# A four-layer transformer block on one core: every other even unit's copy of the transposed probabilities moves from ScalarE to VectorE

## The reference

```python
x = _L0_cond_ref(...)   # RMS norm, 8 query heads on 1 key head, rotary, softmax, gated MLP (silu)
x = _L1_cond_ref(...)   # layer norm, 16 heads of 32 channels, normalised q and k, MLP (gelu)
x = _L2_cond_ref(...)   # layer norm, 16 query heads on 4 key heads, masked attention, no MLP
x = _L3_cond_ref(...)   # 8 experts of 64 channels, layer norm, silu, output projection
```

```python
mask = outside_window & ~global_visible | future_block
scores = jnp.einsum('bhtd,bhsd->bhts', q, k_exp) / jnp.sqrt(HEAD_DIM)
scores = jnp.where(mask, -jnp.inf, scores)
attn = jax.nn.softmax(scores, axis=-1)
y = jnp.einsum('bhts,bhsd->bhtd', attn, v_exp)
```

## Time and profile before

| | |
|---|---|
| median of three runs | 1913.11 us |
| the profiled execution's own time | 1912.22 us |
| its span, first to last instruction | 1910.4 us |
| TensorE (matmul) busy | 1839.4 us, 96% |
| VectorE busy | 1130.7 us, 59% |
| ScalarE busy | 1026.9 us, 54% |
| GpSimd busy | 819.3 us, 43% |
| mean granted TensorE clock | 0.987 of full speed |
| copies `PT<-B` on ScalarE / VectorE | 160 / 128 |

### The profile page before, as it was taken

How to read it: one execution, slowest core, us unless ns; L and a number is a source line. 1 busy time by engine, 2 the same in 40 slices (tenths; PEclk the granted TensorE clock), 3 DMA queues, 4 the chain that set the end, 5 groups by cost and what they waited for, 6 DMA issues and landing times.

```text
span 1910.4 us, 35240 instructions
## 1 busy us (share of the span) xinstructions
PE 1839.4 (96%) x12840; PEld 1480.8 (78%) x12840; DVE 1130.7 (59%) x3224; ACT 1026.9 (54%) x2482; POOL 819.3 (43%) x1094
## 2 busy tenths in 40 slices
PE   5889999999999999999999999999999999989987
PEld 3678778888888888888788888878886878865565
DVE  5867445643553446543775488586475786476563
ACT  3553433532343445443566467477467765559875
POOL 4666662211112344233778565336443442244330
PEclk9999999999999999999999999999999999989989
DMA  7436787556445544445456534623532354422421
GB/s 246 140 122 215 255 292 257 191 196 221 156 171 176 187 167 144 166 160 183 141 172 226 180 144 144 208 102 126 206 122 85 132 193 172 165 83 90 127 73 56
DMA packets 98651, 314.76 MB, mean 165 GB/s; under 512 B 11568, under 2 KB 13232, under 8 KB 96944
## 3 DMA queue, kind: packets, MB, share of 16 engines
q1 hardware_dynamic: 98480, 312.52, 47.2%
HBM read 242.48 MB, written 66.58 MB: 162 GB/s over the span
## 4 chain that ended last, share of the span: by engine, by line
PE 85%; DVE 5%; ACT 4%; POOL 3%; DMA 2%; issue 2%; SPq 0%; DVEq 0%; POOLq 0%; ACTq 0%
PE B L360 78%; PE B L363 7%; POOL W L378 1%; ACT SS L366 1%; DMA ST<-in_wpack 1%; DVE T L378 1%; ACT GF L366 1%; DVE FB L381 1%; POOL W L375 1%; ACT L366 1%; POOL SS L375 1%; POOL FB L378 1%; DMA Y<-in_adaw 0%; DVE Y L378 0%; ACT FB L366 0%
## 5 line engine op out<-in xcount | busy, mean ns | idle before, releaser
L375 POOL TENSOR_SCALAR SS<-SS,NM 128x256 f32<-128x256 f32 (+1 forms) x640 | 298.7, 486 | 620.1 <-DVE NM L390 619.8
L360 PE MATMUL B<-HM,W 128*128 128x512 f32 x2304 | 532.1, 390 | 1.0 <-DVE HM L381 1.0
L360 PEld LDWEIGHTS B<-HM,W 128*128 128x128 f32 x2304 | 431.7, 188 | 91.8 <-DVE HM L381 1.8
L360 PE MATMUL B<-G,W 128*128 128x512 f32 x1536 | 381.6, 398 | 2.8 <-POOL W L378 2.4
L360 PEld LDWEIGHTS B<-G,W 128*128 128x128 f32 x1536 | 280.9, 188 | 64.2 <-issue 3.1
L366 ACT ACTIVATE SS<-SS,NM 128x256 f32<-128x256 f32 (+1 forms) x512 | 240.2, 472 | 72.8 <-DVE NM L384 72.4
L360 PE MATMUL B<-HA,W 128*128 128x512 f32 x864 | 221.0, 405 | 8.7 <-DVE HA L378 4.7
L360 PEld LDWEIGHTS B<-HA,W 128*128 128x128 f32 x864 | 161.7, 192 | 50.5 <-issue 8.7
L363 PE MATMUL B<-ident,SS 128*128 128x128 f32 x1152 | 166.7, 281 | 11.9 <-POOL SS L375 9.6
L378 POOL TENSOR_TENSOR R<-R,few 128x16 f32<-128x16 f32 (+2 forms) x57 | 120.7, 2121 | 126.2 <-DVE R L375 126.2
L363 PEld LDWEIGHTS B<-ident,SS 128*128 128x128 f32 x1152 | 133.8, 143 | 44.7 <-issue 13.4
(11 more groups left out here) (111 smaller groups left out, 2647.2 us busy)
## 6 DMA issues: line engine op xcount, KB each, us to landing
W<-kept SPq DMA_DIRECT2D x357, 512.0 KB, 4.4
kept<-W SPq DMA_DIRECT2D x119, 512.0 KB, 4.9
ST<-in_wpack SPq DMA_DIRECT2D x139, 256.0 KB, 2.9
Y<-in_adaw SPq DMA_DIRECT2D x12, 1024.0 KB, 6.4
FB<-FB SPq DMA_DIRECT2D x52, 64.0 KB, 2.9
X<-in_xT SPq DMA_DIRECT2D x1, 3072.0 KB, 13.2
out_xT<-X SPq DMA_DIRECT2D x12, 256.0 KB, 3.8
FB<-in_pos SPq DMA_DIRECT2D x4, 256.0 KB, 5.0
```

Source lines behind the costliest of these rows:

```text
L360: return self.real.matmul(*a, **k) if self.real is not None else self
L375: return self.real.tensor_scalar(*a, **k) if self.real is not None else self
```

## The change

In the third layer the one copy of an even unit is ScalarE's where `g` is a multiple of four, and VectorE's otherwise. The 64 units of the layer have 32 even ones; 16 of them (`g` = 114, 118, ... 126, 146, ... 190) change engine. Everything else keeps its engine, and no step changes its place in the list.

```diff
+def by_scalar(g, k):
+
+    if layer(g) == 2 and g % 2 == 0:
+        return g % 4 == 0
+    return (k + (0 if layer(g) else g % 2)) % 2 == 0
@@ values, TensorE
-                            e.wait_ge(*(a_pt if (k + (qt if nh == 2 else 0)) % 2 == 0 else d_pt).of(g + qt, k))
+                            e.wait_ge(*(a_pt if by_scalar(g + qt, k) else d_pt).of(g + qt, k))
@@ copy, VectorE
-                    if (k + (0 if layer(g) else g % 2)) % 2:
+                    if not by_scalar(g, k):
@@ copy, ScalarE
-                    if (k + (0 if layer(g) else g % 2)) % 2 == 0:
+                    if by_scalar(g, k):
```

## The result

The changed kernel takes 1916.26 us (median of 16 runs, 1912.58 to 1921.06), the kernel before beside it 1912.03 us (16 runs, 1907.40 to 1914.43). The ratio is 1.0025, 95% interval 1.0017 to 1.0033: slower by some 4.8 us (the medians lie 4.2 us apart). The prediction was 1914.1 us, with a range of 1910.0 to 1918.5. The time lies in the range, but past the 1915.7 at which the forecast's own case ended, and slower by over 0.2% is the outcome to which I gave 0.18. The range was right; the net of +1.0 us was not.

What follows compares the result with a forecast made beforehand. TensorE, busy 96% of the span, bounds the kernel, so only its waits count. Losses of 1.9 us less gains of 0.9 give net +1.0 us: 1914.1 us expected, 8-in-10 range 1910.0 to 1918.5.

Steps and rivals of the forecast that it cites:

- the forecast's own case: Whole kernel: net -0.5 to +2.5 us with the clock unchanged, range 1912.5 to 1915.7 us, chance 0.60.
- unit 170's 0.1: VectorE would end unit 170's copy at 1721.76, TensorE starts the bank's next use at 1721.70: +0.1 us.
- the prediction's own signs of being wrong: TensorE's waits for VectorE's PT up over 1 us, half-clock stretches differing in number or length, or time outside 1912.5 to 1915.7.
- 166: Unit 166: the copy delays VectorE's two T<-T, for which TensorE's B<-few,T at 1702.75 waits; +0.55 us.
- 174: Unit 174: the copy delays VectorE's three T<-T, for which TensorE's B<-few,T at 1757.42 waits; +0.5 us.
- 170: Unit 170: ScalarE's exponentials, table load and gelus come earlier, shortening TensorE's wait at 1725.65; -0.48 us.
- VectorE's next wait for TensorE swallows the 0.6: At nine units (114, 122, 126, 146, 154, 158, 162, 178, 190) the copy's delay on VectorE was to reach nothing: 0.
- unit 182's "-0.43; if they don't, 0": Earlier gelus bring B<-T,few at 1816.94 forward 0.43 us if transposes waiting for GpSimd's late multiplies fit ahead; otherwise 0.
- unit 150's +0.34: The copy ahead of VectorE's HM row at 1549.73 delays the last HM row and the matmuls on it: +0.34 us.
- Unit 118: The copy leaves some 0.1 us through the masked maxima ahead of a later copy: +0.1 us.
- unit 186's +0.28: VectorE's late FB<-Y,B delays B<-ZH,W at 1834.56 by 0.48 us, partly absorbed in the later ZL wait: +0.28 us.
- Rival 1: TensorE's clock falls once more, likely at 1749 to 1758 or 1710 to 1716: 1918.1 us if long, 1915.5 short; chance 0.22.

Runs made afterwards that it cites:

- eleven: Against the kernel before, the moved copies except those of units 166, 174, 178, 182 and 186 go to VectorE; 1912.49 us, ratio 1.0002.
- last8: Against the kernel before, only the eight late copies, units 162 to 190, go to VectorE; 1914.34 us, ratio 1.0015.
- five: Against the kernel before, only the copies of units 166, 174, 178, 182 and 186 go to VectorE; 1916.61 us, ratio 1.0016.
- only182: Against the kernel before, unit 182's copy alone goes to VectorE; 1910.26 us, one execution.
- load: Against the kernel before, ScalarE keeps all copies and VectorE does an extra unread 128x512 maximum at each of the 16 places; 1915.76 us, ratio 1.0017.
- relief: Against the kernel before, the 16 copies are left out on both engines, with TensorE's waits for them; 1911.77 us, ratio 0.9998.
- pair: Against the kernel before, VectorE gets unit 170's copy in its place and unit 182's behind the cast of Q and the CX row; 1910.94 us, ratio 0.9996.
- only186: Against the kernel before, unit 186's copy alone goes to VectorE; 1913.72 us, one execution.
- the single units: Three kernels, each moving one copy to VectorE against the kernel before: unit 178, 182 or 186; 1913.79, 1910.26 and 1913.72 us, one execution each.
- behind182: Against the kernel before, unit 182's copy alone goes to VectorE, behind the cast of Q, the reciprocals and the CX row; 1914.38 us, one execution.

## Why the prediction was right and wrong

**What bounds the kernel** held. Unit 122's tight bank held, and unit 170's 0.1 came and was swallowed by the wait for GF behind it. Besides that no matmul waited anew for VectorE's PT; two weight loads did, at 1751 and 1815 us, by 0.87 and 0.81 us, and no matmul was late for it. The 11 places of "eleven" together cost nothing that could be measured. That the time lies in the range is in part luck: its upper part was there for one more half-clock stretch between 1700 and 1800 us, which did not come. Two of the prediction's own signs of being wrong came, the time past 1915.7 and half-clock stretches of another length.

**Right in mechanism and size:** 166 (+0.55 said, +0.60 measured, both in last8 and five too), 174 (+0.5, +0.58), 170 (-0.48, -0.47).

**The step that failed first: "VectorE's next wait for TensorE swallows the 0.6".** I counted 178 among the nine units of which I said this. The late instruction there was no maximum of scores but an FB for which ScalarE was waiting already. ScalarE had no slack behind it, and the delay came out 17 us later on TensorE: +0.50 at 1789.20. Following VectorE's queue was not enough; the engine that waits for it had to be followed until it had idle time to spare.

**The second: unit 182's "-0.43; if they don't, 0".** The early side was right (-0.47 in only182). The multiplies were 0.5 late as said, but slower as well, at 0.8 us for 0.37, so they did not "just fit", and the bound "0" left out that a collision can cost. Measured +0.56 in the changed kernel, of which the copy makes 0.30 (only182, five) and VectorE's pause the rest. That it is delay and slowing together is shown by only182, load, relief and pair against each other.

**The third: unit 150's +0.34.** VectorE's delay was sized well (+0.39 in load, 0.3 for the HM rows of the changed kernel). What failed is the condition of the sum, "with the clock as it was": the half-clock stretch began 0.9 us later in the list, and TensorE did not wait for HM at all. It is the one error on the other side, and it is luck: in an execution whose stretch begins as before, the loss is to be expected. Unit 118 was mis-sized: +0.36 for +0.1, and it is VectorE's, since load has it and relief not.

**The fourth: unit 186's +0.28.** The delay ahead of ZH,W is 0.44 to 0.46 us (load, only186, after); I let part of it vanish in the later wait for ZL. That wait did vanish, but the clock stayed low 3.4 us longer.

**The clock.** Rival 1 was one more stretch of half clock between 1700 and 1800. None came: the wait of 0.78 us fell into the stretch that was there and did not lengthen it, and that of 0.66 us brought no new one. What came is longer stretches near 1826 and 1891. The steps of the copies that load, relief and the single units show are 0.36 + 0.60 - 0.47 + 0.58 + 0.50 + 0.30 + 0.45 = 2.3 us; VectorE's pause at unit 182 adds 0.26, and unit 150 up to 0.3 more where the clock leaves it its loss. The ratio says 4.8 us (3.2 to 6.3).

How much of the rest is the clock can be bounded by the mean granted clock that each execution has on record. It averages 0.9838 over the 16 executions of the changed kernel and 0.9849 over the 75 of the kernel before that ran beside the experiments, and their mean times are 4.1 us apart (the 16 of the kernel before that ran beside the changed one, for which no clock is recorded, were 0.7 us faster than those 75). A straight line through all executions, with one slope for all kernels, gives 0.58 us for each 0.001 of clock (standard error 0.07). By it the lower clock makes 0.6 us, and at equal clock the changed kernel is still 3.5 us slower (standard error 0.5) and load, with a mean clock of 0.9857, 3.4 us. By the prediction's price, 0.42 us for each us at half clock, 0.0011 of clock is some 4.1 us at half clock and 1.7 us, and leaves 2.4. So the larger part of the loss is not that the clock was low for longer. The first figure leaves some 1 us that the steps and the pause do not account for, the second nothing; no run here tells which holds. Where a low stretch begins counts too: it gives 0.6 us to the HM rows at unit 150 and takes 0.45 at unit 186.

## What to carry to other kernels

When a copy moves to a less busy engine, price each place by who is queued behind it and follow the delay through the engine that waits for it until it meets idle time that is not waiting for the delayed work itself; 11 of these 16 copies together cost nothing that could be measured, the five others a ratio of 1.0016. Check also what will now run at the same time: a late and an early instruction can meet, and "it just fits" then has a cost above zero. A copy whose place costs something may be free four instructions later in the same queue, as unit 182's was.

## What the runs showed of the hardware

GpSimd's multiply of 128x128 elements (SBUF to SBUF) takes 0.37 us alone and 0.80 to 0.90 us beside VectorE's additions with two SBUF inputs. Both sides can be slowed: VectorE's T<-Y took 0.82 us where it began while a multiply ran (pair, relief), and 0.69 where it began just ahead of one, which then took 0.90 (only182). I had not looked for this in the kernel before, where one multiply of the four shows it.

TensorE's half-clock stretches differ between kernels with the same matmul list: some have one of 3.4 us at 1411, 1710 or 1750 and others none, and near 1826 they have 10.2 to 20.5 us in all (behind182 and last8 have the most). In the kernel before the clock fell at 1546.1, 1699.7 and 1826.0, and in the 10 us ahead of each TensorE was never idle for longer than 0.62, 0.78 and 0.90 us. A single execution can't settle a question of 1 us in this kernel; the steps of the same matmul can.
